# Fixed-operand multiplies on TensorE around the end of attention and at the opening of the fused stage

## What is computed

```python
x = x + tanh(g_xattn) * attention(layernorm(x), ctx, Wq, Wk, Wv, Wout, bout)   # 8 heads of 64, context of 77
x = x + tanh(g_ffn) * ffn(layernorm(x), Wg, W1, W2, Ws1, Ws2)

def ffn(x):                       # 16 experts of 128, the best 2 per token, plus a shared MLP of 256
    scores = softmax(x @ Wg.T); wk, idx = top_k(scores, 2)
    z  = sum over the 2 experts of wk * (u * silu(g)) @ W2[e]      # u, g = split(x @ W1[e])
    ys = (u * silu(g)) @ Ws2                                       # u, g = split(x @ Ws1)
    return z + ys
```

## Time and profile before

| | us |
|---|---|
| median of 3 runs | 992.02 (991.86 to 994.16) |
| the profiled execution | 994.32 |
| its span, first to last instruction | 992.5 |
| `attend` ends, `mix` opens (TensorE) | 495.98 |
| `mix` ends, `passes` opens (TensorE) | 714.70 |

### The profile page before, as it was taken

The page is one execution under the profiler, slowest core; times in us unless marked ns, Lnnn a source line. Parts: engine busy times, 40 slices in busy tenths (PEclk is TensorE's granted clock), DMA queues, the critical chain, the costliest instruction groups (busy, mean ns, idle before and its releaser), DMA issues. The chain is left out here.

```text
span 992.5 us, 20889 instructions
## 1 busy us (share of the span) xinstructions
PE 919.1 (93%) x6722; PEld 854.1 (86%) x6722; DVE 806.0 (81%) x1840; ACT 524.2 (53%) x1191; POOL 495.0 (50%) x604
## 2 busy tenths in 40 slices
PE   6699999999999999999779999998797889899994
PEld 6599999999999999998768888887597889699993
DVE  7899999999999999988568989988476568278773
ACT  6577776777777775644254455553043334144441
POOL 4346354453645355343434555554346457457765
PEclk9799999999999999999779999999999889999997
DMA  8213323332233222221153444443799998478880
GB/s 238 73 47 105 91 61 92 92 105 66 86 92 105 71 68 72 70 71 44 38 192 107 171 168 164 169 161 121 273 317 350 336 353 279 148 256 269 264 279 27
DMA packets 108342, 151.15 MB, mean 152 GB/s; under 512 B 21830, under 2 KB 72394, under 8 KB 108240
## 3 DMA queue, kind: packets, MB, share of 16 engines
q1 hardware_dynamic: 92880, 107.60, 35.0%
q0 software_dynamic: 15360, 42.24, 11.2%
HBM read 90.19 MB, written 65.90 MB: 157 GB/s over the span
## 5 line engine op out<-in xcount | busy, mean ns | idle before, releaser
L671 POOL TENSOR_TENSOR prob<-prob,row_sum 128x616 f32<-128x616 f32 x64 | 77.9, 1217 | 141.9 <-DVE row_sum L893 141.9
L1527 POOL DMA_INDIRECT rows_scratch<-prow x80 | 78.7, 984 | 66.2 <-DVE prow L1666 37.2
L1116 POOL DMA_INDIRECT rows_scratch<-row,slot x64 | 67.9, 1061 | 75.4 <-DVE row L1367 60.7
L1527 POOL DMA_INDIRECT out<-prow x80 | 78.7, 984 | 49.7 <-issue 26.8
L1624 ACT ACTIVATE eyT_hi<-ps_ey 128x512 fp32r<-128x512 f32 x80 | 47.9, 599 | 105.2 <-PE ps_ey L1549 105.2
L75 PE MATMUL ps_h<-w_flat,eyT_hi 128*128 x320 | 97.5, 305 | 0.0
L1649 DVE TENSOR_TENSOR eyT_lo<-ps_ey,eyT_hi 128x512 fp32r<-128x512 f32 x80 | 55.3, 692 | 49.0 <-ACT eyT_hi L1624 46.2
L76 PE MATMUL ps_h<-w_flat,eyT_hi 128*128 x320 | 90.6, 283 | 0.0
L77 PE MATMUL ps_h<-w_flat,eyT_lo 128*128 x320 | 90.5, 283 | 0.0
L75 PE MATMUL ps_s<-M_hi,xT_hi 128*128 128x308 f32 x256 | 82.0, 320 | 7.4 <-PEq L387 4.1
L805 ACT ACTIVATE prob<-prob,rstd 128x616 f32<-128x616 f32 x64 | 51.9, 811 | 67.4 <-DVE prob L883 67.4
(11 more groups left out here) (283 smaller groups left out, 3338.8 us busy)
## 6 DMA issues: line engine op xcount, KB each, us to landing
prow<-rows_scratch SPq DMA_DIRECT2D x160, 258.0 KB, 3.6
rows_scratch<-blank SPq DMA_DIRECT2D x34, 258.0 KB, 3.8
xT_raw<-in_xT SPq DMA_DIRECT2D x32, 256.0 KB, 4.5
x_tok<-in_x SPq DMA_DIRECT2D x32, 256.0 KB, 2.8
x_scratch<-x_tok SPq DMA_DIRECT2D x32, 256.0 KB, 3.1
row<-x_scratch SPq DMA_DIRECT2D x16, 512.0 KB, 3.9
x_ahead<-in_x SPq DMA_DIRECT2D x26, 256.0 KB, 4.4
w_raw<-in_W SPq DMA_DIRECT2D x16, 256.0 KB, 3.5
```

The costliest lines, as they stand in the source:

```text
L671: nc.gpsimd.tensor_tensor(pr, pr, row_sum[i][:, :].unsqueeze(2).broadcast_to((P, H, CK)), ALU.mult).then_inc(normed, 1)
L1116: pool.indirect_dma_start(c.rows1, bass.IndirectOffsetOnAxis(slot1[:, t:t + 1], 0), row[G % NX][:, i, :], None).then_inc(scattered[G % NX] ...
L1527: pool.indirect_dma_start(dram, bass.IndirectOffsetOnAxis(target, 0), row[u][:, i, 0:columns], None, bounds_check=bound, oob_is_err=False) ...
```

## The change

Three calls of `busy` are added after the loop of `attend`, each with the bias tile (128x256, fp32) as the moving operand and `ps_proj[1]` as the bank: 9 multiplies ahead of `attend_values(31)`, 7 ahead of `project_out(31)` and 7 behind it. The call that opens `mix` goes from 6 multiplies (128x384) to 16.

```diff
@@ -778,8 +778,12 @@
                         transpose_probs(b, 1)
 
                 groups(pe, body)
+                spare = ps_proj[1]
+                busy(nc, c, spare, c.bias[:, :], 9)
                 attend_values(B - 1)
+                busy(nc, c, spare, c.bias[:, :], 7)
                 project_out(B - 1)
+                busy(nc, c, spare, c.bias[:, :], 7)
 
             def V_out(s):
                 return V[s][0:CK, :, 0:4:3, :]
@@ -1184,7 +1188,7 @@
-                busy(nc, c, ps_h[0], c.stats2[:, :], 6)
+                busy(nc, c, ps_h[0], c.stats2[:, :], 16)
                 transpose_y(0)
                 pe.wait_ge(wg_ready, 1)
                 score(0)
```

## The result

| | kernel before | changed kernel |
|---|---|---|
| median of 20 runs each (lowest to highest) | 992.38 us (989.10 to 996.54) | 996.14 us (993.12 to 1000.05) |
| ratio, 95% interval | | 1.0043 [1.0028, 1.0057] |
| profiled execution, its span | 994.32, 992.5 | 996.77, 995.0 |
| mean granted clock of it | 0.967 | 0.974 |

A forecast was written before the change was run, and what follows sets the result against it. TensorE bounds the fused stage, so the start of score(1) decides: barrier, sixteen multiplies and a renewed clock fall make it 4.2 us late. Carried to the median, 992.02 + 4.2 = 996.2 us, range 993.6 to 998.9.

The forecast's parts named there:

- Price: Cost of one 256-wide fp32 filling multiply, scaled by columns from 0.65 us for 384: 0.433 us, give or take 0.04.
- Rival (c): A filling multiply costs one record's time, so fills fit their pauses; score(1) 4 to 6 us early, 986 to 988; chance 0.06.
- Fills 1 and 2: Last batch: fills hold the clock; values start 1.6 us late, gain 0.7; projection starts 0.7 late, its result gains 0.8.
- (d): Rival: the fills do not hold the clock at all; barrier 10 us or more late, 1002 us; chance 0.04.
- Fill 3 and the barrier: End of attention: TensorE's drain waits for the queued fill and becomes last, barrier 1.3 us late (0.4 to 2.2).
- Fill 4: Opening of mix, sixteen multiplies, 10.4 us: first transposes 5.3 us late, second transposes 3.9 late, set by ScalarE's rows.
- The clock behind fill 4: Between sixteen multiplies and score(1): clock falls again, hidden(0,0) takes 4.36 to 5.8 us, score(1) 3.9 to 6.5 late, 4.2 taken.
- Rival (a): Clock holds behind the sixteen multiplies; VectorE may delay score(1); +1.8 to +3.0 us, 993.8 to 995.0; chance 0.27.
- From score(1) to the end: Rest of fused stage and passes: nothing takes the 4.2 us back; the passes only shift.
- The step from one execution to the median: The profiled execution's 4.2 us added unchanged to the median of the runs: 992.02 + 4.2 = 996.2 us.
- (b): Rival: the last batch's clock fall is not in the typical run; change pays 4.2 + 2.3, 998.5 us; chance 0.17.
- the rule for single long gaps: Skill page's rule blaming clock falls on idle gaps longer than any pause here; would favour a held clock; given little weight.

The follow-up runs named there:

- third_only: Changed kernel cut to its seven multiplies behind the last projection, opening of mix back at 6; 995.71 us, ratio 1.0015 to the kernel before.
- before_again: Kernel before, unchanged, run and profiled a second time, its profile left out of the table; 993.23 us, ratio 0.9988.
- before: Kernel before, unchanged, its first profile; median 992.38 us, profiled execution 994.32.
- before_third: Kernel before, unchanged, a third profile; 991.88 us.
- after: The whole change, its first profile; median 996.14 us, ratio 1.0043 to the kernel before, profiled execution 996.77.
- after_again: The whole change run again with a second profile; 996.97 us, ratio 1.0059 to the kernel before.
- open_only: Kernel before with nine multiplies instead of six opening mix and three more behind the first transposes; 992.08 us, ratio 0.9996.
- rounded: Changed kernel with its attention fills (9, 7, 7) as single-record multiplies of rounded operands and 9 at the opening; 990.67 us, ratio 1.0007 to the kernel before.
- over12: Changed kernel without the fill behind the last projection and with 9 multiplies opening mix; 993.68 us, ratio 1.0027 to the kernel before.
- fit_t: Kernel before with 4, 3, 0 multiplies around the last batch, 9 opening mix, 3 behind the first transposes; 991.03 us, ratio 0.9982.
- attn_only: Changed kernel with its three attention fills (9, 7, 7) alone, mix opening with 6 as before; 996.60 us, ratio 1.0040 to the kernel before.

## Why the prediction was right, point by point

The time, 996.14 for 996.2, and the sign were right. The sum behind them had one term too large and left out one that it had priced as a rival; the two cancel, so that a forecast within 0.1 us is luck. Times are again counted from the last transposes.

**Price.** Right. The first fill's 18 records start at 481.33 and the values at 485.03: 3.70 for nine, 0.411 each, against 0.433 ± 0.04. The 384-wide ones: 10.39 for sixteen, 0.65 as taken. Rival (c) is out.

**Fills 1 and 2.** Right in kind: values 1.42 late (predicted 1.6), the projection 0.43 late (0.7), its last result 0.98 early (0.8): 493.87 + 0.28 - 480.40 = 13.75 against 14.73. The clock held through all of it, so (d) is out.

**Fill 3 and the barrier.** Right: TensorE's drain became the last, mix opens 0.94 late against the profiled execution before (1.3), inside the stated 0.4 to 2.2. third_only shows the mechanism by itself.

**Fill 4.** Right: first transposes 4.94 late (5.3), with no wait before them, second transposes 3.68 late (3.9), still set by ScalarE's rows (0.52 of idle before them).

**The clock behind fill 4: the term that was mis-sized.** The fall came where it was said to, at 513.1 behind the full-clock score. But it lasted to 516.5 alone. I had hidden(0,0) at 4.36 to 5.8, with a lower end read from a row whose own low stretch reached from 503.5 to 513.7; it took 3.68. From rank to score(1) it was 1.53 instead of 1.68. Score(1) is 2.82 late, not 4.2. Rival (a) had priced about that, up to 3.0, for another reason that did not happen: the clock did fall, and VectorE's small operation took 0.16 at 516.02 and was not held up beside GpSimd's split at 516.58.

**From score(1) to the end.** "Nothing takes it back" was right within 1 us: 995.0 - 519.99 = 475.0 against 992.5 - 516.51 = 476.0. Within the fused stage nothing was taken back at all: counted as in the table, the first transposes of the passes start at 242.09 against 238.90 (718.64), 3.2 late; it is the passes that were 1.4 shorter, less than they differ between executions of one code. So the profiled executions differ by 0.66 + 2.82 - 0.98 = 2.5, not 4.2.

**The step from one execution to the median: the step that failed.** I carried the difference of one profiled execution to the median unchanged and gave (b) 0.17. (b) is half true. An execution without the fall opens mix at 12.42; against that the change is 4.76 late at the opening, 8.69 at the first transposes (27.57 against 18.88) and 6.4 at score(1) (39.59 against 33.21), where (b) had put 6.5. With two of five executions like the profiled one and three like the other, 0.4 x 2.8 + 0.6 x 6.4 = 5.0, and with half and half (before_again counted) 4.6, against 2.8 to 5.7 measured. The weights rest on five or six profiles, three of them of the kernel before itself; the remaining difference can lie there, or in low stretches right behind score(1), which differ from execution to execution (before and before_third have none there, after none and after_again one of 6.8 us). That part stays open. (b) as a time, 998.5, was too high.

There was a hint in the page that I read, though a weak one: the profiled execution was 2.3 above the median of its runs, and I treated that as an offset and not as a possible sign that the row under study was one of two kinds. Weak, because the twenty runs spread over 7 us and the passes alone differ by more than 2.3.

## What to carry to other kernels

In this kernel a fill against a falling clock paid only where it ended before the operands arrived: the same idea cost 4.3 us with fills that overrun their pauses by 1.4 to 4 us, and won 4.1 with fills that fit, two of them in pauses that the change had left alone. Fitting is not enough by itself, as open_only and rounded show no measured gain. Put none ahead of a block's end, where TensorE's drain waits for it, and follow the clock on to the next pause, since a held stretch can simply fall there. And profile the kernel before at least twice before taking a fall of the clock as the cost to be removed; in this case it was in two executions of five, or three of six with before_again.

## What the runs showed of the hardware

**The fall is not set by the instruction stream alone.** The same pauses of 2.11 and 1.41 us went with a fall in two profiles of the table (and in before_again) and with none in three, and in open_only the clock fell at 487.2, between values that follow one another without a pause. In the opening it is steadier: all of the ten profiles in the table with nothing between the first transposes and the score have a fall there, 0.8 to 6.0 us after these transposes begin (500.7 against 499.91 in before_third, 513.2 against 507.19 in after_again); the three with a fill there have none before rank(0), a split that chance alone gives in 1 of 286 cases. At this place the fills did hold the clock. The Trainium skill, page "TensorE: Matmul & The Clock Gate", section "What's actually happening", says that the number of multiplies that run before the clock rises varies from run to run of the same kernel. The traces show the like for the fall: 3.2 us after the last transposes began in before, 4.4 in before_again, 5.1 in open_only, and none in before_third.

**No long pause came ahead of the falls.** No pause of TensorE ahead of the falls in the table was longer than 2.94 us (over12). The Trainium skill, same page, section "A second HAM failure mode: psum-queue depth-cycling", tells of a clock that falls under frequent short idles between groups of multiplies; the traces here are nearer to that than to the rule for single long gaps that the prediction weighed, though some of the falls followed one or two pauses only (2.11 us in before).

**Dense work at the low level.** Once low, the clock stayed low through dense multiplies: in the windows above for 9.9 us in fit_t, 8.79 of them busy, for 10.1 in attn_only, 9.09 busy, and for 6.3 in after_again without any idle time. The low stretches of the table are 3.4 to 10.3 us long. What a fall costs is therefore not in the pause but in the work behind it.
